# A two-layer decoder kernel: a reordered entry, a clamp on 16-bit data, query weights centred on GpSimd, gate weights as the stationary operand

## The reference

```python
x = x + L0_attn(ln(x))    # quantised state-space block
x = x + L0_xattn(ln(x), ctx)   # 16 heads of 128
x = x + L0_ffn(ln(x))     # 8 experts, top 2, weights from atoms and a sparse table
x = x + L1_attn(ln(x))    # channels attend to channels (512 x 512)
x = x + L1_xattn(ln(x), ctx)   # 16 heads of 32, queries and keys layer-normalised
x = x + L1_ffn(ln(x))     # 12 experts, top 2
...
def qa(x, s): return clip(round(x / s), -128, 127)
def qw(w):    s = max(abs(w)) / 127; return clip(round(w / s), -128, 127), s
...
x_q = qa(ln(x), 0.05); wq, ws = qw(in_proj_w)
proj_q = qa(x_q @ wq.T * (0.05 * ws), 0.02)          # hs_q, gate_q
u_q = qa(silu(conv(hs_q, cwq) * (0.02 * cws) + conv_b), 0.01)
...
def _ln(t, w, b): return (t - mean(t)) * rsqrt(var(t) + 1e-6) * w + b   # per head, L1_xattn
```

## Time and profile before

| what | value |
|---|---|
| median of 3 runs | 3809.16 us (3806.95 to 3812.80) |
| the profiled run | 3798.11 us |
| its span | 3796.40 us |
| PE busy | 3303.2 us, 87% of the span |
| DVE busy | 2493.5 us, 66% |
| ACT busy | 1766.4 us, 47% |
| POOL busy | 1207.5 us, 32% |
| mean granted PE clock | 0.933 |

### The profile page before, as it was taken

One profiled execution on the slowest core, in us unless ns is written; L12 is line 12 of the kernel. 1 busy time (PEld: TensorE's weight loads), 2 busy tenths in 40 slices (PEclk: granted clock), 3 DMA queues, 4 the chain that ended last, 5 costly groups with the idle time before them and its releaser, 6 DMA issues. The chain is left out here.

```text
span 3796.4 us, 38397 instructions
## 1 busy us (share of the span) xinstructions
PE 3303.2 (87%) x12729; PEld 1722.7 (45%) x12741; DVE 2493.5 (66%) x4700; ACT 1766.4 (47%) x3318; POOL 1207.5 (32%) x927
## 2 busy tenths in 40 slices
PE   2751499999999799999999999899899779999964
PEld 2330144444444354554555454544444446555552
DVE  7768899999999565555555555533311458777554
ACT  3657566666666243343344333343201237677521
POOL 0243599999998010010000000124580010000014
PEclk9885699999999899999999999799999889999957
DMA  6114434343432222212211111446420110000046
GB/s 214 69 57 135 161 96 137 103 136 105 129 110 67 93 75 64 81 64 73 67 55 55 53 59 34 145 136 210 143 91 3 51 66 1 1 1 1 4 140 218
DMA packets 199893, 332.28 MB, mean 88 GB/s; under 512 B 25488, under 2 KB 76048, under 8 KB 196624
## 3 DMA queue, kind: packets, MB, share of 16 engines
q1 hardware_dynamic: 186624, 296.09, 23.9%
q0 software_dynamic: 12208, 33.57, 3.2%
q10 hardware_dynamic: 864, 0.18, 0.0%
HBM read 216.38 MB, written 113.38 MB: 87 GB/s over the span
## 5 line engine op out<-in xcount | busy, mean ns | idle before, releaser
L1201 POOL TENSOR_TENSOR sc_dBu<-sc_dtu,xa 128x1024 f32<-128x1024 f32 x256 | 539.9, 2131 | 41.2 <-DMA sc_dtu<-scan_dtu 32.0
L1111 PE MATMUL y_ps<-sc_g,ident 128*128 128x512 f32 x1024 | 476.3, 600 | 18.4 <-POOL sc_g L1189 12.0
L1225 DVE TENSOR_TENSOR_SCAN sc_dA<-sc_dA,sc_dBu 128x1024 f32<-128x1024 f32 x160 | 365.1, 2282 | 6.3 <-POOL sc_dBu L1201 6.3
L1451 ACT ACTIVATE c_p<-c_ps,c_sm 128x512 f32<-128x512 f32 x256 | 195.6, 774 | 353.4 <-DVE c_sm L1492 353.4
L1165 ACT ACTIVATE sc_dA<-sc_dt,a_neg 128x511 f32<-128x511 f32 x512 | 329.5, 676 | 11.0 <-DVE sc_g L1225 9.8
L1491 DVE TENSOR_REDUCE c_sm<-c_ps 128x4 f32<-128x2048 f32 x64 | 146.7, 2292 | 275.6 <-PE c_ps L1414 275.6
L1111 PEld LDWEIGHTS y_ps<-sc_g,ident 128*128 128x128 f32 x1024 | 189.8, 190 | 256.5 <-issue 168.1
L1484 DVE SCALAR_TENSOR_TENSOR xa<-c_ps,c_sm,xa 128x512 f32<-128x512 f32 x256 | 192.1, 751 | 146.3 <-PE c_ps L1405 132.7
L1405 PE MATMUL c_ps<-c_wo,c_oT 128*128 128x512 f32 x512 | 246.5, 605 | 2.3 <-DVE xa L1484 1.6
L1386 PE MATMUL c_ps<-c_xT,c_wq 128*128 128x512 f32 x512 | 232.3, 597 | 5.3 <-DMA c_wq<-in_c_wq_dram 5.3
L1433 PE MATMUL c_ps<-c_pT,c_v 128*128 128x512 f32 x512 | 232.1, 596 | 1.7 <-DVE c_pT L1503 1.7
(11 more groups left out here) (496 smaller groups left out, 6421.8 us busy)
## 6 DMA issues: line engine op xcount, KB each, us to landing
kv_w<-in_c_wkv_dram SPq DMA_DIRECT2D x32, 512.0 KB, 4.1
cross_keys<-kv_out SPq DMA_DIRECT2D x64, 256.0 KB, 2.0
cross_values<-kv_out SPq DMA_DIRECT2D x128, 128.0 KB, 1.9
c_kT<-cross_keys SPq DMA_DIRECT2D x64, 256.0 KB
c_rk<-cross_rk SPq DMA_DIRECT2D x64, 256.0 KB
c_v<-cross_values SPq DMA_DIRECT2D x64, 256.0 KB
expert_rows<-e_yt SPq DMA_DIRECT2D x63, 256.0 KB, 2.0
xa<-scan_bc SPq DMA_DIRECT2D x48, 256.0 KB, 7.6
```

The costliest lines, as they stand in the source:

```text
L1111: ins = pe.matmul(yps[:, k % 2, :], ident[:], g[:, c % GS, n, :], start=False, stop=(m == NCH - 1 and n == NG - 1))
L1201: pool.tensor_tensor(dBu[:, c % 3], spread(dtu[:, k % DT, :], NG), bc[:, m * NG:(m + 1) * NG, :], ALU.mult).then_inc(s_dBu, 1)
L1225: dve.tensor_tensor_scan(to.rearrange("p n s -> p (n s)"), dA[:, c % 2].rearrange("p n s -> p (n s)"), dBu[:, c % 3].rearrange("p n s -> p ...
L1451: ins = act.activation(pr[:, j, :], ps[:, SB + j, :], ACT.Exp, scale=rq[:, j:j + 1], bias=bias[:, j:j + 1], accum_out=l[:, j:j + 1])
```

## The change

- `rsqrt` runs three iterations instead of four, except in the entry and in `x_proj`.
- `entry`: SP's transfers stand in another order, small ones go to ACT's queue; DVE waits for `cw` alone ahead of its widest value; the comparison and `awT` stand ahead of the first quantised chunk; the statistics of the first eight tiles stand behind it; `sp_wt` stands between the second and third chunk, ACT's sigmoid behind its second; POOL's select also waits for the first chunk. The rounding loop rounds fp32 to bf16 (`xb`) and then clamps in bf16; the transposes are bf16. The raw x_proj, dt_proj and out_proj weights are loaded here, their widest values found in the loop, and their reduction over partitions is POOL's last instruction.
- `in_proj_conv`: those loads, `widest` and the reduction are gone; `scales` follows the first step, the quantising stands a step earlier. Each step's first pass takes off the constant and bounds from above with a bf16 result, the second bounds from below, in place.
- `norm_all`: the gate weights are the stationary operand and 512 columns of `xT` move, once in four tiles; DVE copies the result (`kept`), PE transposes it back (`placed`).
- `experts0`: six instead of eight products ahead of the tiles; the load of the third batch's context moves behind the tiles.
- `attn1`, `qkv1`: POOL centres the four tiles of query weights and their bias after the keys and SP stores them to HBM; the norm of `cross1` loads them from there. `centre` is gone from `qkv1`; PE projects two blocks and then turns keys and queries of a block, one after the other.

```diff
-def rsqrt(dve, own, r, v, t):
+def rsqrt(dve, own, r, v, t, steps=3):
 
     own.after(dve.tensor_scalar(t.bitcast(I32), v.bitcast(I32), 1, None, ALU.logical_shift_right))
     own.after(dve.tensor_scalar(r.bitcast(I32), t.bitcast(I32), -1.0, float(0x5F3759DF), ALU.mult, ALU.add))
-    for _ in range(4):
+    for _ in range(steps):
...
-                def logits(t):
-                    gw, _, lps = gate
-                    ne = gw.shape[2]
-                    if t == 0:
+                def logits(b):
+                    gw = gate[0]
+                    if b == 0:
                         pe.wait_ge(s_gw, 16)
-                    copied(t)
+                    if b >= 2:
+                        pe.wait_ge(s_le, b - 1)
+                    for t in range(b * TT, (b + 1) * TT):
+                        copied(t)
                     for c in range(HC):
-                        pe.matmul(lps[:, t * ne:(t + 1) * ne], xT[:, c, t * P:(t + 1) * P], gw[:, c, :],
-                                  start=(c == 0), stop=(c == HC - 1))
+                        ins = pe.matmul(gps[:, b % 2, :], gw[:, c, :], xT[:, c, b * S:(b + 1) * S], start=(c == 0),
+                                        stop=(c == HC - 1))
+                    ins.then_inc(s_lg, 1)
+
+                def placed(b):
+                    pe.wait_ge(s_le, b + 1)
+                    for t in range(b * TT, (b + 1) * TT):
+                        pe.transpose(gate[2][:, t * ne:(t + 1) * ne], lgT[:, b % 2, t % TT * P:(t % TT + 1) * P],
+                                     ident[0:ne, 0:ne])
...
+                    if gate is not None and t >= 6 and (t - 6) % TT == 0:
+                        logits((t - 6) // TT)
+                    if gate is not None and t >= 8 and t % TT == 0:
+                        placed(t // TT - 2)
                 if gate is not None:
-                    for t in range(NT - 3, NT):
-                        logits(t)
+                    logits(NB - 1)
+                    placed(NB - 2)
+                    placed(NB - 1)
...
-                sp.dma_start(aw[:], A["eaw"]).then_inc(s_aw, 16)
-                sp.dma_start(idx[:], A["mask_idxT"]).then_inc(s_idx, 16)
                 sp.dma_start(idxb, A["mask_idx"].partition_broadcast(P)).then_inc(s_idxb, 16)
+                sp.dma_start(atoms[:], A["atoms"]).then_inc(s_atoms, 16)
+                sp.dma_start(imp[:], A["importanceT"].rearrange("(i p) e -> p i e", p=P)).then_inc(s_imp, 16)
                 for b in range(NB):
                     sp.dma_start(xa[:, b * TT:(b + 1) * TT, :], x_dram[:, b * TT:(b + 1) * TT, :]).then_inc(s_x[b], 16)
-                sp.dma_start(atoms[:], A["atoms"]).then_inc(s_atoms, 16)
-                sp.dma_start(imp[:], A["importanceT"].rearrange("(i p) e -> p i e", p=P)).then_inc(s_imp, 16)
+                sp.dma_start(raw_x.rearrange("p (c n) -> p c n", c=CT),
+                             A["x_proj_wT"].rearrange("(c p) n -> p c n", p=P)).then_inc(s_lx, 16)
+                sp.dma_start(raw_dt, A["dt_proj_wT"]).then_inc(s_ldt, 16)
...
+                sp.wait_ge(s_done, HC)
+                sp.dma_start(raw_out.rearrange("p (c n) -> p c n", c=CT),
+                             A["out_proj_wT"].rearrange("(c p) n -> p c n", p=P)).then_inc(s_lout, 16)
+                sp.wait_ge(s_small, 80)
...
                 pool.wait_ge(s_eq, 1)
+                pool.wait_ge(s_done, 1)
 
                 pool.affine_select(out=low, in_=eq[:], compare_op=ALU.is_gt, fill=0.0, base=0,
                                    pattern=[[0, ST], [-1, P]], channel_multiplier=1).then_inc(s_low, 1)
+                pool.wait_ge(s_mx2, 1)
+                pool.partition_all_reduce(mxa[:], mx[:], P, ABSMAX)
...
-                act.wait_ge(s_small, 96)
-                act.activation(a_neg[:], alog[:], ACT.Exp).then_inc(s_exp, 1)
                 act.wait_ge(s_inv, 1)
                 for i in range(HC):
                     if i >= 2:
                         act.wait_ge(s_done, i - 1)
                     integer(i, near[:, i % 2, :], raw[:, i * WC:(i + 1) * WC], W_IN)
+                    if i == 1:
+                        act.wait_ge(s_small, 80)
+                        act.activation(a_neg[:], alog[:], ACT.Exp).then_inc(s_exp, 1)
+                        act.wait_ge(s_imp, 16)
+                        act.activation(imp[:], imp[:], ACT.Sigmoid).then_inc(s_sig, 1)
...
-                dve.wait_ge(s_small, 96)
+                dve.wait_ge(s_cw, 16)
...
-                quantized(0, near[:, 0, :], raw[:, 0:WC], W_IN, wq[:, 0, :])
                 dve.wait_ge(s_idxb, 16)
                 dve.tensor_tensor(eq[:], along(idxf[:], P), idxb.rearrange("p (i q) -> p i q", q=P),
                                   ALU.is_equal).then_inc(s_eq, 1)
                 dve.wait_ge(s_atr, 1)
                 dve.tensor_copy(awT[:], ip[0:NATOM, 0, 0:NE0]).then_inc(s_awT, 1)
+                quantized(0, near[:, 0, :], raw[:, 0:WC], W_IN, wq[:, 0, :])
+                stats(0)
+                stats(1)
                 quantized(1, near[:, 1, :], raw[:, WC:2 * WC], W_IN, wq[:, 1, :])
-                stats(0)
+                dve.wait_ge(s_del, 1)
+                dve.wait_ge(s_sig, 1)
+                dve.tensor_tensor(wt[:].rearrange("p i e -> p (i e)"), ip[:, 1, 0:ST * NE0],
+                                  imp[:].rearrange("p i e -> p (i e)"), ALU.mult).then_inc(s_wt, 1)
                 quantized(2, near[:, 0, :], raw[:, 2 * WC:3 * WC], W_IN, wq[:, 2, :])
-                stats(1)
+                stats(2)
...
+                widest = {3: (W_X, raw_x, s_lx), 6: (W_DT, raw_dt, s_ldt), 10: (4, raw_out[:, 0:QCH], s_lout),
+                          13: (5, raw_out[:, QCH:2 * QCH], s_lout)}
                 for t in range(NT + 2):
                     if t < NT:
                         dve.wait_ge(s_ap, t + 1)
-                        v = xn[:, t % R, :]
-                        own.after(dve.tensor_scalar(v, v, -128.0, 127.0, ALU.max, ALU.min))
-                        dve.tensor_scalar(v, v, MAGIC, MAGIC, ALU.add, ALU.subtract).then_inc(s_xn, 1)
+                        v = xb[:, t % R, :]
+                        if t >= R:
+                            dve.wait_ge(s_tr, t - R + 1)
+                        own.after(dve.tensor_scalar(v, xn[:, t % 2, :], MAGIC, MAGIC, ALU.add, ALU.subtract))
+                        dve.tensor_scalar(v, v, -128.0, 127.0, ALU.max, ALU.min).then_inc(s_xn, 1)
...
+                    if t in widest:
+                        w, x, s_load = widest[t]
+                        dve.wait_ge(s_load, 16)
+                        ins = dve.tensor_reduce(mx[:, w:w + 1], x, AX_X, ALU.max, apply_absolute_value=True)
+                    if t == 13:
+                        own.after(ins)
+                        dve.tensor_tensor(mx[:, W_OUT:W_OUT + 1], mx[:, 4:5], mx[:, 5:6], ALU.max).then_inc(s_mx2, 1)
...
-                extra = {0: widest, 1: scales, 4: lambda: remainder(0), 5: lambda: quantized(0), 6: lambda: remainder(1),
-                         7: lambda: quantized(1), 9: lambda: remainder(2), 10: lambda: quantized(2),
+                extra = {0: scales, 3: lambda: remainder(0), 4: lambda: quantized(0), 5: lambda: remainder(1),
+                         6: lambda: quantized(1), 8: lambda: remainder(2), 9: lambda: quantized(2),
                          16: lambda: remainder(3), 17: lambda: quantized(3)}
...
-                    own.after(dve.tensor_scalar(v, v, MAGIC - 128.0, MAGIC + 127.0, ALU.max, ALU.min))
                     if what == "hs":
-                        ins = dve.tensor_scalar(hs[:, i, :, PAD:PAD + S], v.rearrange("p (b s) -> p b s", b=NB), MAGIC, None,
-                                                ALU.subtract)
+                        to, v = hs[:, i, :, PAD:PAD + S], v.rearrange("p (b s) -> p b s", b=NB)
                     else:
-                        dst = gate if what == "gate" else u
-                        ins = dve.tensor_scalar(dst[:, i, :], v, MAGIC, None, ALU.subtract)
-                    ins.then_inc(s_d, 1)
+                        to = (gate if what == "gate" else u)[:, i, :]
+                    own.after(dve.tensor_scalar(to, v, MAGIC, 127.0, ALU.subtract, ALU.min))
+                    dve.tensor_scalar(to, to, -128.0, None, ALU.max).then_inc(s_d, 1)
...
-EARLY = (2, 6, 8)
+EARLY = (2, 6, 6)
...
+                    elif t < KV + HC:
+                        sp.dma_start(kb[:, q, :], A["c1_wq"][(t - KV) * P:(t - KV + 1) * P, :]).then_inc(s_kl[q], 16)
+                    else:
+                        sp.dma_start(kb[:, q, :], A["c1_bq"].partition_broadcast(P)).then_inc(s_kl[q], 16)
...
+                    if t >= KV:
+                        pool.tensor_tensor(heads, heads, along(mean[:], HD), ALU.subtract).then_inc(s_kd, 1)
+                        pool.wait_ge(s_kd, t + 1)
+                        continue
...
-            keyed(0)
-            own.after(centre(bq[:], NH1))
```

(5 more changed lines are left out.)

185 lines of the change are left out of this document (85 added, 100 removed).

## The result

| | before | new |
|---|---|---|
| median | 3808.05 us (4 runs, 3794.75 to 3812.80) | 3741.19 us (4 runs, 3736.67 to 3748.27) |
| profiled run | 3798.11 us | 3736.67 us |
| its span | 3796.40 us | 3734.90 us |
| mean granted PE clock | 0.933 | 0.948 |

The ratio is 0.9837, with a 95% interval of 0.9808 to 0.9865. Forecast were 3755 and 3733 to 3782. Between the two spans lie 61.5 us, where 54.6 were forecast.

A forecast was written before the change was run, and what follows sets the result against it. Each section between all-engine barriers was taken as bound by its last engine. Entry -16.6, projection -22, roots -3, logits -7, first experts +2, query weights -8 sum to -54.6, so 3809.16 becomes 3755 us, range 3733 to 3782.

The forecast's parts named there:

- first four steps: Entry: DVE waits for `cw` alone -2.85, comparison moved -1.85, select beside statistics -3.44, `sp_wt` two chunks earlier -12.48 us.
- The second group is covered: Five norms: only the first group's shorter root saves time, -0.6 us each, -3.0 in all.
- The bound of -12: Gate logits in the two gated norms: the largest gain allowed, at full clock in both, beside the forecast -7 us.
- The lead of 5.5: First experts: with two products fewer ahead of them, the tiles can start some 5.5 us earlier.
- The early start: qkv1: with query weights already centred, PE's first projection starts with the section, 14.0 us earlier.
- Left at 0: Long sections (scan, first cross attention, self attention, heads): they keep their bounds, so their change was costed at 0.
- the forecast's own sign: Whole kernel: the forecast is wrong if a section left at 0 moves, or PE's clock falls in long sections.
- the projection that gains only its head: Rival, input projection: -13 us in place of -22, total 3764 us; chance 0.15.
- the half clock in the gated norms: Rival, gate logits: PE stays at half clock, +8 us in place of -7, total 3770 us; chance 0.13.
- the moved stall: Rival, entry: DVE waits for `sp_wt`'s inputs between chunks, the 12.5 us come back, total 3767 us; chance 0.08.
- the stretched cells: Rival, input projection: cells take 14.0 us each, +58.6 in place of -22, total 3835 us; chance 0.02.
- the case in which all covers hold: Rival, projection and gated norms: cells end near 109 us, logits at full clock, total 3740 us; chance 0.07.

The follow-up runs named there:

- late_and_four: New kernel with the sparse product back ahead of the rounding loop and four iterations in every reciprocal root; entry 112.6 us, 12.2 more than in the new kernel's first trace.
- second pair: Traces of the unchanged kernel before and the new kernel, both taken again on one other chip; their section differences sum to -53.6 us, against -61.5 in the first pair.
- before_again: The kernel before, unchanged, run and traced once more on another chip; gated norms 50.2 and 40.8 us, first experts 237.5 us.
- turns_back: New kernel with the old order of turns in qkv1 (keys two blocks ahead, queries one behind); that section 85.9 us, from 91.7.
- third group: Last of three groups of runs, on the second chip, with kernel before and new kernel run again unchanged; medians 3791.8 and 3733.6 us.
- gates_back: New kernel with the gate logits as they were (transposed tile stationary, 8 or 12 columns moving); median 3748.4 us, 14.8 over the new kernel beside it.
- cells_11: New kernel with 11 cell updates in the input projection in place of 14; that section 113.8 us, the next grew from 47.0 to 51.4.

## Why the prediction was right, and where its terms were not

The sign and the range held: -54.6 forecast, -61.5 measured in the first pair of traces, -53.6 in the second. The order of the terms did not: the gate logits gave twice what the query weights gave, and the sum owes its closeness in part to errors of opposite sign. Taken by its own steps:

- **Entry, -16.6 forecast, -19.0 measured.** Every one of the first four steps is in the rows. Up to the loop 8.1 us were forecast (2.85 + 1.85 + 3.44) and 8.6 measured (84.73 to 76.16). The stall of 12.48 is gone, and `late_and_four` brings 11.6 to 12.2 of it back. Mis-sized was the loop: +3.8 forecast, +1.9 measured (76.16 to 97.8). DVE's six copies read 16-bit data now and take 0.42 instead of 0.69, which the working had at the old price; that is 1.6 of the 1.9.
- **The select beside the statistics.** The select took 3.84 us there instead of 5.96, and four statistics took 2.47 beside it (34.87) and 2.47 without it (57.63). The Trainium skill (SBUF — State Buffer, Who interferes with whom) says that a DVE operation with one SBUF input outside the 2-port modes doesn't contend with GpSimd. The trace agrees.
- **Input projection, -22 and -22.0.** The number is right by luck. The second pair gives -18.2, and all traces together -18.0 to -22.1 (135.1 and 137.2 before, 115.0 to 117.1 new). The first step is borne out: the cells start with the section. The 16-bit pass takes 0.69 us, not the 0.94 that I scaled from a row of another shape; the Trainium skill (VectorE: DVE Perf Modes, The perf-mode tier table) states 693 ns, and the trace agrees to the nanosecond or two (694). By that the cells would have ended at 110 and the engines at some 109, and the term would be -25. Two things ate the 3 us. In the first trace the last cell took 3.8 us longer to its landing than the last one before the change (8.9 for 5.1), mostly because its scatter landed late; it ran beside the store of the last gate tile. In most other traces that store itself ends the section, and I had left it out: in the kernel before it ended well under the cells. The pass that I had too dear and the end that I had too cheap cancelled.
- **Roots, -3.0 forecast, about -3.3 measured.** "The second group is covered" held but for 0.15 us: at equal clock an ungated norm loses 0.7 us, a gated one 0.6, which makes 3 x 0.7 + 2 x 0.6 = 3.3. The first pair has 1.3 for each ungated norm, the second 1.9 for the three together; up to 0.6 of a norm's difference is TensorE's clock in its last transposes, which the forecast had left out.
- **Gate logits, -7 forecast, -15.8 measured** (-4.8 and -11.0, with the roots taken off). This is the term that was off most, and the step that failed is the size of the gain at full clock: I had 13.8 less for PE in the second norm and gave back more than half of it for the end and for other bounds. But the other bounds weren't there: an ungated norm takes 25.7, and the last group, its copy and the eight small transposes add 12.9 to it together with what the groups before push back. The bound of -12 was too near as well, because I took the state of the clock in one trace for a property of the kernel. In `before_again` the same two norms lie at 50.2 and 40.8; against that pair the term would be -11.0 and -1.6, -12.6 in all.
- **First experts, +2 forecast, +7.6 in the first comparison, +4 to +5 in the others.** The added 6.9 + 0.9 are right. The lead of 5.5 is the term that was mis-sized: 5.3 at the first tile, 3.5 at the last, because PE waits 4.72 for the gather and then does the first product below full clock (5.32 for 3.67). That makes 4.2, as the second pair has it (+4.3). Some 3.3 more are a gap in one execution.
- **Query weights, -8 forecast, -7.6 and -5.7 measured.** The early start gave 13.3 us and not 14.0: the first projection stood at 3041.73 in a section that starts at 3028.42. The blocks' periods were forecast 16.3, 21.0 and 20.4; the first two projections took 27.70 together, and then the starts lie 22.1 and 21.0 apart (3022.99 less the 13.9 before it, and 3043.95). The cost of the new order, forecast 4.4 + 1.6, is what `turns_back` gives back: 5.8, or 6.6 in the third group.
- **Left at 0.** The rest is 2.8 us longer in the first pair and the heads are 2.4 shorter; in the second pair it is +1.3 and -0.3. The rest lies within what the new kernel's traces have among themselves (2548.7 to 2552.3); for the heads two traces of the kernel before are too few to say. By the forecast's own sign, a section left at 0 that moves, the first pair alone would have spoken against it.

Of the rivals, the projection that gains only its head, the half clock in the gated norms, the moved stall and the stretched cells did not come. Nearest to the outcome was the case in which all covers hold (3740), but for another reason than it named: the cells were not at 109; the entry and the clock gave more. Its sum also needs the entry's bound of -20, which it doesn't name; with the two bounds that it names it is 3744.

## What to carry to other kernels

Where sections end at barriers, cut the span there first, list every engine and every queue that ends late in a section, stores included, and forecast each section by the latest of them. Before a move that starts work earlier, look at what it will wait for at the new place: the tiles of the first experts found their gather not landed, the turns their bank not emptied, and both of those edits were better undone (11.1 us). If a trace shows a stretch of small matmuls at half clock, take a second trace before you size the gain, and try to exchange the two operands so that the long one moves. And take a second pair of traces before you call a term confirmed: here rows moved by up to 9 us between two pairs of the same kernels, more than most terms are large.

## What the runs showed of the hardware

- PE worked without a pause on records of 8 or 12 moving columns between transposes, and its granted clock fell from 1.00 to 0.50 after 3.4 us (`gates_back`), 6.8 (first trace of the kernel before) or 10.3 (`before_again`), or never rose (one norm in each of the last two). With 128 or 512 moving columns and the roles exchanged it rose to 1.00 between 11.9 and 15.5 us into the norm and stayed there to its end in twenty of twenty-two such norms of eleven traces. In the other two (`turns_back`, `cells_11`) it was at half for another 3.4 us around the first group, which then took 4.8 us for 3.6, and the norm 40.2 for 38.6.
- The kernel before spreads over 15.9 us in the six runs of the last group (3783.0 to 3798.9), the new kernel over 4.4 in four (3731.8 to 3736.3), but over 11.6 in its first four (3736.7 to 3748.3). With the old gate logits alone put back the spread is 4.1, so the gates don't explain the whole of it.
- An indirect gather, an add and a scatter of 128 rows, issued by GpSimd, took 5.4 us with the other engines quiet, 7.4 to 7.8 beside DVE passes that held 46 us of the section, and 8.0 to 8.3 beside passes that held 59. A last scatter landed in 2.1 us in the kernel before and in 4.4 beside a store of 1 MB.
